# Self-attention in a fused network on Trainium2: row maxima sent in halves, the first quarter's high maxima made in its steps, k's first transfers on POOL's queue, half of the last batch finished in its steps

## The reference

```python
K = jnp.einsum('bse,hed->bhsd', xk, Wk)
V = jnp.einsum('bse,hed->bhsd', xv, Wv)
Q = jnp.einsum('bqe,hed->bhqd', xq, Wq)
scores = jnp.einsum('bhqd,bhkd->bhqk', Q, K)
scores = jnp.where(causal, -jnp.inf, scores)
att = jax.nn.softmax(scores / jnp.sqrt(jnp.asarray(sk, scores.dtype)), axis=-1)
out = jnp.einsum('bhqk,bhkd->bhqd', att, V)
...
return jax.nn.relu(out @ Wo + bo)
```

## Time and profile before

| | us |
|---|---|
| median of 3 runs | 2786.29 (2785.91 to 2787.86) |
| profiled execution | 2794.9 |
| its span | 2793.1 |
| PE busy | 2454.3 (88%) |
| DVE busy | 1614.1 (58%) |
| ACT busy | 1289.4 (46%) |
| POOL busy | 1321.1 (47%) |
| mean granted TensorE clock | 0.944 |
| self-attention, from its first instruction to the next stage's | 1042.4 to 1832.1 of the span |

### The profile page before, as it was taken

How to read it: one execution, slowest core, us unless ns; L and a number is a source line. 1 busy time by engine, 2 the same in 40 slices (tenths; PEclk the granted TensorE clock), 3 DMA queues, 4 the chain that set the end, 5 groups by cost and what they waited for, 6 DMA issues and landing times. The chain is left out here.

```text
span 2793.1 us, 42845 instructions
## 1 busy us (share of the span) xinstructions
PE 2454.3 (88%) x12770; PEld 1434.9 (51%) x12771; DVE 1614.1 (58%) x3230; ACT 1289.4 (46%) x2555; POOL 1321.1 (47%) x2216
## 2 busy tenths in 40 slices
...
DMA packets 85048, 115.13 MB, mean 41 GB/s; under 512 B 13880, under 2 KB 64160, under 8 KB 83072
## 3 DMA queue, kind: packets, MB, share of 16 engines
...
## 5 line engine op out<-in xcount | busy, mean ns | idle before, releaser
L3275 ACT ACTIVATE L2S_pT<-L2S_t_ps 128x512 f32<-128x512 f32 (+3 forms) x768 | 356.2, 490 | 251.4 <-PE L2S_t_ps L3102 243.9
L3339 DVE TENSOR_REDUCE L2S_mx<-L2S_s_ps 128x1 f32<-128x768 f32 (+7 forms) x384 | 351.4, 952 | 142.2 <-PE L2S_s_ps L3031 139.6
L3562 POOL TENSOR_SCALAR_AFFINE_SELECT L2S_pT<-L2S_pT 128x128 f32<-128x128 f32 x512 | 154.2, 310 | 374.9 <-ACT L2S_pT L3275 370.4
L3102 PE MATMUL L2S_t_ps<-L2S_q,L2S_k 98*128 98x512 bf16 (+3 forms) x768 | 254.5, 346 | 40.5 <-ACT L2S_pT L3275 24.1
L3030 PE MATMUL L2S_s_ps<-L2S_k,L2S_q 96*128 96x512 bf16 (+3 forms) x768 | 208.0, 344 | 29.7 <-DVE L2S_mx L3339 20.4
L622 POOL TENSOR_TENSOR L_prob<-L_prob,L_rc 128x616 f32<-128x616 f32 x64 | 82.3, 1287 | 231.3 <-DVE L_rc L555 231.3
L3102 PEld LDWEIGHTS L2S_t_ps<-L2S_q,L2S_k 98*128 98x128 bf16 x768 | 73.0, 99 | 227.1 <-ACT L2S_pT L3275 153.3
L3941 DVE TENSOR_TENSOR L3B_h<-L3B_si,L3B_u_ps 128x512 f32<-128x512 f32 x71 | 48.8, 688 | 237.9 <-PE L3B_u_ps L3884 213.0
L3858 POOL DMA_INDIRECT out<-L3B_y,L3F_rows x71 | 114.8, 1618 | 132.7 <-DVE L3B_y L3947 120.2
L3183 PE MATMUL L2S_o_ps<-L2S_pT,L2S_v 128*32 128x512 f32 (+3 forms) x1536 | 172.5, 524 | 0.0
L319 PE MATMUL L_scores<-weights,L_xT 128*128 128x308 f32 x512 | 143.1, 423 | 2.3 <-ACT L_xT L442 1.6
...
## 6 DMA issues: line engine op xcount, KB each, us to landing
...
```

The lines of the kernel that those rows point to most:

```text
L3102: nc.tensor.matmul(o[:, lo:512], k6[:, q % 2, j, kt * P:(kt + 1) * P], q6[:, q % 2, j, c * 512 + lo:(c + 1) * 512], start=True, stop=True) ...
L3275: nc.scalar.activation(pT[:, st % SLOTS, j, lo:512], t_ps[j % 2][:, lo:512], ACT.Exp, scale=SK).then_inc(s["exp_done"], 1)
L3339: nc.vector.tensor_reduce(dst, src, AX.X, ALU.max).then_inc(s["mx_done"], 1)
L3562: nc.gpsimd.affine_select(out=edge, in_=edge, compare_op=ALU.is_ge, fill=0.0, base=0, pattern=[[1, P]], channel_multiplier=-1).then_inc(s[ ...
```

## The change

1. `mx`, `mrow`, `q6` are laid out in two halves (low 512 queries, high 512), and `turn_max` has a half: the low half of the next quarter is turned at step 7, unit 3, the high half at step 1, unit 1 of the quarter itself. PE waits for the rows of a half only at that half's first unit (step 0, step 4).
2. In the prologue only the eight low maxima of quarter (0,0) are made; its sixteen high ones stand in steps 0 to 3 of the quarter, one per unit, and its high turn at step 3, unit 3. In that quarter the maxima of the next one go into steps 4 to 11, three each (FIRST_SHARE).
3. SHARE moves maxima from steps 6 and 7 to step 10. TURN_X moves by two units, PROJECT from steps (1: 5, 6, 8, 9; 2: 0, 3, 5, 8) to (1: 6, 8, 9, 11; 2: 5, 6, 8, 9).
4. k's first six writes and its first six loads are issued by POOL; SP waits for the writes before its loads of q. POOL's memset of k's rows of ones waits for all of xn instead of rstd.
5. In the last batch tiles 0 to 3 are transposed and multiplied by Wo at quarter 3, steps 8 to 11 (`end_turn`, `end_finish`), with residual and statistics by DVE; their rstd comes first in `last_walk`, their normalising after the last output turn, their scale and shift on POOL; they are sent by themselves. The end handles tiles 4 to 7.

The diff, cut to its core:

```diff
-    SHARE = (2, 2, 2, 2, 3, 3, 3, 3, 2, 2, 0, 0)
+    SHARE = (2, 2, 2, 2, 3, 3, 2, 2, 2, 2, 2, 0)
+    FIRST_SHARE = (0, 0, 0, 0, 3, 3, 3, 3, 3, 3, 3, 3)
     PEAK_AT = {0: (), 2: (0, 1), 3: (0, 1, 2)}
+    LAST_TURN_A = ((3, 8, 1), (3, 9, 1))
+    LAST_FINISH = ((3, 10), (3, 11))
     STATS = ((0, 1), (0, 3))
     NORM = ((1, 1), (1, 2))
-    TURN_X = ((1, 3, 0), (1, 3, 2), (1, 4, 0), (1, 4, 2))
-    PROJECT = ((1, 5), (1, 6), (1, 8), (1, 9), (2, 0), (2, 3), (2, 5), (2, 8))
+    TURN_X = ((1, 3, 2), (1, 4, 0), (1, 4, 2), (1, 5, 0))
+    PROJECT = ((1, 6), (1, 8), (1, 9), (1, 11), (2, 5), (2, 6), (2, 8), (2, 9))
...
-        q6 = sb("q6", [MR, 2, 4, S], BF16)
+        q6 = sb("q6", [MR, 2, 2, 4, 512], BF16)
...
-        mx = sb("mx", [P, 2, 4, TB])
-        mrow = sb("mrow", [4 * TB, 2, P], BF16)
+        mx = sb("mx", [P, 2, 2, 4, 4])
+        mrow = sb("mrow", [16, 2, 2, P], BF16)
...
-                    share, peaks = peaks[:SHARE[st]], peaks[SHARE[st]:]
+                    m = (FIRST_SHARE if first and q == 0 else SHARE)[st]
+                    share, peaks = peaks[:m], peaks[m:]
                     at = (q, st)
                     for j in range(4):
                         unit(q, st, j)
-                        for n, place in zip(share, PEAK_AT[SHARE[st]]):
+                        if first and q == 0 and st < 4:
+                            peak(0, TB + 4 * st + j)
+                        for n, place in zip(share, PEAK_AT[m]):
                             if place == j:
                                 peak(q + 1, n)
                         if (st, j) == (2, 2) and (q or not first):
                             turn_out(q - 1, 1)
                         if (st, j) == (7, 0):
                             turn_out(q, 0)
-                        if (st, j) == (10, 1) and (q + 1 < QUADS or more):
-                            turn_max(q + 1)
+                        if (st, j) == (7, 3) and (q + 1 < QUADS or more):
+                            turn_max(q + 1, 0)
+                        if (q, st, j) == (0, 3, 3) and first or (st, j) == (1, 1) and (q or not first):
+                            turn_max(q, 1)
...
+                        if not more:
+                            if (q, st, j) in LAST_TURN_A:
+                                end_turn(LAST_TURN_A.index((q, st, j)))
+                            if at in LAST_FINISH and j in (1, 2):
+                                end_finish(LAST_FINISH.index(at), j - 1)
...
-            for n in range(NP):
+            for n in range(TB):
                 peak(0, n)
-                if 1 <= n <= TB:
-                    first_v(n - 1)
-            turn_max(0)
+                first_v(n)
+            turn_max(0, 0)
...
+                sp.sem_inc(s["loaded_low0"], 48)
+                sp.sem_inc(s["loaded_high0"], 48)
                 write(0, 0, 0, 2)
-                write(0, 0, 1, 3)
+                sp.wait_ge(s["k_written"], 96)
+                sp.sem_inc(s["written1"], 96)
                 written(0, 0)
                 for q in range(2):
                     for cols, n in ((lowc, "low"), (highc, "high")):
-                        for which in "qk":
+                        for which in "qk" if q else "q":
...
+                for half, done in ((0, "a_half"), (1, "a_last")):
+                    sp.wait_ge(s[done], 1)
+                    chip.settle(sp)
+                    at = (B - 1) * TB + 4 * half
+                    sp.dma_start(dram["a"][:, at:at + 4, :], att[:, 4 * half:4 * half + 4, :]).then_inc(s["a_out"], 16)
+                sp.wait_ge(s["a_out"], 16 * B + 16)
...
+            def max_turned(q, half):
+                nc.tensor.transpose(r_ps[0:16, 0:P], mx[:, q % 2, half].rearrange("p h i -> p (h i)"), chip.ident[:]).then_inc(s["r_full"], 1)
...
-                    if st == 0 and j == 0:
-                        pe.wait_ge(s["mrow_in"], 32 * QUADS * b + 32 * (q + 1))
+                    if kt == 0 and j == 0:
+                        pe.wait_ge(s[f"mrow_in{c}"], 32 * QUADS * b + 32 * (q + 1))
...
+                def end_turn(dh):
+                    r.freed(pe, ("ea", dh))
+                    pe.wait_ge(s["r_dve"], r.dve(r.order.index(("o", QUADS - 1, 0)) + 1))
+                    for i in range(4):
+                        mm = nc.tensor.transpose(r_ps[:, i * P:(i + 1) * P], att[:, i, dh * P:(dh + 1) * P], chip.ident[:])
+                    mm.then_inc(s["r_full"], 1)
+
+                def end_finish(g, half):
+                    if half == 0:
+                        r.freed(pe, ("ef", g))
+                    if g == 0 and half == 0:
+                        pe.wait_ge(s["r_act"], r.act(r.order.index(("ea", 1)) + 1))
+                    for k in range(KD):
+                        t = 2 * g + half
+                        mm = nc.tensor.matmul(r_ps[:, half * D:(half + 1) * D], attT[:, k, t * P:(t + 1) * P], w["L2S_Wo"][:, k, :],
+                                              start=(k == 0), stop=(k == KD - 1))
+                    if half:
+                        mm.then_inc(s["r_full"], 1)
...
+                            mm = nc.tensor.transpose(s_ps[0][:, (4 * dh + i) * P:(4 * dh + i + 1) * P], att[:, 4 + i, dh * P:(dh + 1) * P], chip.ident[:])
+                    mm.then_inc(s["pre_full"], 1)
+                    pe.wait_ge(s["act_pre"], 11)
+                    for i in range(4):
+                        for k in range(KD):
+                            mm = nc.tensor.matmul(s_ps[1][:, i * D:(i + 1) * D], attT[:, k, (4 + i) * P:(5 + i) * P], w["L2S_Wo"][:, k, :],
+                                                  start=(k == 0), stop=(k == KD - 1))
+                        if i % 2:
+                            mm.then_inc(s["pre_full"], 1)
...
+                    dve.wait_ge(s["r_full"], r.full(("ef", g)))
+                    nc.vector.tensor_tensor(t, r_ps[:].rearrange("p (i d) -> p i d", d=D),
+                                            wide(chip.vec("L2_xattn_bo1").unsqueeze(1), [P, 2, D]), ALU.add).then_inc(s["r_dve"], 1)
+                    dve.wait_ge(s["r_dve"], r.dve(r.order.index(("ef", g)) + 1))
+                    dve.wait_ge(s["res_done"], 4 * B)
+                    rest_and_stats(t, 2 * g, end_step)
...
+                    pool.wait_ge(s["xn_done"], TB)
...
+                def project(m):
+                    if m:
+                        return
+                    pool.wait_ge(s["split_done"], 3)
+                    chip.settle(pool)
+                    for p in range(3):
+                        for qq in range(2):
+                            nc.gpsimd.dma_start(dram["parts"][1:2, qq, 2 - p, :, :, :].rearrange("o d h s -> (o d) h s"),
+                                                part[64 * qq:64 * qq + 64, 1, p, :]).then_inc(s["k_written"], 16)
+                    pool.wait_ge(s["k_written"], 96)
+                    chip.settle(pool)
+                    src = dram["parts"][1:2]
+                    for cols, n in ((slice(0, S // 2), 0), (slice(S // 2, S), 1)):
+                        for slot, count, p in ((0, 3, 0), (3, 2, 1), (5, 1, 2)):
+                            nc.gpsimd.dma_start(k6[slot * HD:(slot + count) * HD, 0, :, cols],
+                                                src[:, 0, p:p + count, :, :, cols].rearrange("o p d h s -> (o p d) h s")).then_inc(s[f"k_loaded{n}"], 16)
...
+                    pool.wait_ge(s["norm_y_done"], 2 * B - 1)
+                    chip.settle(pool)
+                    t = att[:, 0:4, :]
+                    nc.gpsimd.tensor_tensor(t, t, wide(chip.vec("L2_xattn_g1").unsqueeze(1), [P, 4, D]), ALU.mult).then_inc(s["scaled"], 1)
+                    pool.wait_ge(s["scaled"], 4 * B + 1)
+                    nc.gpsimd.tensor_tensor(t, t, wide(chip.vec("L2_xattn_b1").unsqueeze(1), [P, 4, D]), ALU.add).then_inc(s["a_half"], 1)
+                    power(rs_y, ve_y, mv_y, 1e-6, "stats_y_done", B + 1, "ve_y_done", "rstd_y_done", slice(4, 8))
```

191 lines of the change are left out of this document (103 added, 88 removed).

## The result

| | before | after |
|---|---|---|
| median, us | 2787.07 (4 runs, 2785.91 to 2791.12) | 2721.48 (4 runs, 2720.32 to 2722.98) |
| profiled execution, us | 2794.9 | 2722.25 |
| self-attention in it, us | 789.7 | 716.4 |
| mean granted clock | 0.944 | 0.957 |

The ratio is 0.9762, 95% interval 0.9746 to 0.9779: 65.6 us faster, where 37.9 were forecast. All of it is in the stage: 73.3 us less there in the profiled executions, 2.9 less ahead of it and 3.6 more behind. The difference of 7 us is spread over the stage, and most of it goes with the granted clock.

The account below looks back on a forecast made before the run. PE was taken to set the pace, joined by DVE where maxima are dense. -6.2 - 0.4 - 0.7 - 16.4 - 11 - 3.2 = -37.9 us (A to F) gave 2748.4 us, range 2738 to 2762, 8 in 10 2732 to 2771.

Parts of the forecast that it names:

- D: Quarters 2: later projections and turns of x end ACT's wait for SP's writes, -16.4 us, range -20 to -8.
- F: Last batch, half finished in its steps: end about 10 us shorter, steps +7, net -3.2 us, range -9 to +1.
- E: Quarters after the first: new shares and half turns give -11 us, range -20 to 0, with 4 set aside for r_ps.
- A: Prologue: with POOL's memset behind xn_done, eight normalising instructions take 3.2 instead of 9.4 us: -6.2, range -6.5 to -4.
- B: Prologue: k's first transfers on POOL's queue bring the first product of maxima -0.4 us, range -2.5 to +2.
- C: First quarter: high maxima moved into its steps, -15.7 + 11.7 + 3.3 = -0.7 us, range -7 to +7.
- (1): Rival: half the gain, D's stall moves to steps 5 and 6 and E gives nothing; -18.5, 2768 us, chance 0.19.
- (2): Rival: denser work in the half-clock stretches gets 2.4 GHz; C -7, D -20, F -9; 2733 us, chance 0.12.
- (3): Rival, slower: each of thirty-one turns waits for r_ps; decides from 2.5 us a quarter, at 2.9 2792 us; chance 0.05.
- (4): Rival: quarter 0 just moves its sixteen maxima, C +7 and B +2; -27.8, 2758 us, chance 0.62 together with the forecast.

Follow-up runs that it names:

- b_moved: Kernel before with only the new places of projections and turns of x (PROJECT, TURN_X): 2741.90 us, ratio 0.9859.
- b_again: Kernel before, unchanged, run once more for a second profile: 2783.53 us, with 782.6 us in the stage instead of 789.7.
- a_early_ones: Changed kernel with POOL's memset of k's rows of ones waiting for rstd again: 2730.07 us, ratio 0.9810.
- b_step2: Kernel before with the second half's projections moved from steps 0, 3, 5, 8 to 3, 5, 6, 8 of quarter 2: 2756.65 us, ratio 0.9903.
- b_both: Kernel before with the projection move of b_step2 and POOL's scale moved from quarter 2 to quarter 3: 2754.47 us, ratio 0.9895.
- b_clear: b_moved with POOL's scale and shift of the batch before moved from quarter 2 to quarter 3: 2738.07 us, ratio 0.9833.
- a_old_end: Changed kernel with the old end, all eight tiles of the last batch finished there in one transfer: 2730.13 us, ratio 0.9806.

## Why the forecast was too small

The direction was right; one step, D, was sized at under half, one term of F was three times too large and lay behind a difference of the clock, and E's sum was right by luck. By the stretches of the first section, with E read off as the difference between b_moved and the changed kernel (560.7 to 551.0):

| part | forecast | shown |
|---|---|---|
| A, B, C | -7.3 | -9.1 |
| D | -16.4 | -38.6 |
| E, with the collision that it took away | -11 | -9.7 |
| F, steps | +7 | -4.4 (at equal clock +2.3) |
| F, end | -10.2 | -11.5 (-10.4 from b_again) |

- **A** was right: 9.43 us of normalising are 2.67, and by a_early_ones the first unit moves by the same 6.7.
- **B** was right, by a cancelling of two things: POOL's issues (0.58 us, inside 0.5 to 0.9) are as many as SP's, and the first product now waits for q. The later first product costs nothing at the first unit. Of what the prediction cites from the Trainium skill (SBUF — State Buffer, the box on the "DVE blocks DMA" trap), that POOL's descriptors can't be written while a DVE instruction runs in a two-port mode, the trace shows nothing: six loads were issued in 3.46 us beside one cast of q's split (0.69 us), the six writes, with no DVE instruction beside them, in 3.45.
- **C** was right in both terms: first unit 22.3 us earlier forecast with A and B, 23.6 measured; quarter (0,0) +15.0 forecast, +14.5 measured. PE's wait at step 4 was 1.86 us, where a gap of 3 to 5 was expected.
- **D is the step that failed: "Its wait goes: -16.4 for three batches", with the range -20 to -8.** It took the wait's own row for the price of the stall, and the stall for all that the new places change. b_step2 shows 3.7, 8.5 and 10.1 us for the three stalls, 22.3 and not 16.4: in the two long ones steps 0 and 1 were 8.2 and 7.9 us longer, and part of what ran behind them did so at a lower clock (1.8 us in step 2 of (1,2)). The collision of split and scale, which the prediction named as what is "late next", was in the kernel before already (3.3 and 2.0 us on top in b_both), and is gone in the changed kernel, whose (1,2) takes 39.59. And "the moves (1,5) to (1,11) cost nothing" was wrong the other way: the first three quarters 1 got 9.1 us shorter in b_moved, 7.5 against b_again, in (1,1) at steps 3, 5 and 6 (0.8, 1.2 and 0.9 us). No run takes apart why. Two lengths in the trace had hinted at the size: quarter (1,2) takes 54.16 us, (3,2), with the same score work and nothing besides, 32.9. The excess of 21 us should have been shared out among its causes, the projections' own work too, before one of them was given 6.5; after the change 7.1 of it are left (39.59 against 32.51).
- The Trainium skill (SBUF — State Buffer, "Practical consequences") says that a cast can enter a two-port mode, in which it and a GpSimd instruction block each other, and that a tensor_tensor with both inputs in SBUF contends with a GpSimd instruction that reads SBUF. b_moved's trace agrees (0.43 becomes 1.14, 0.69 becomes 1.64); the prediction used the rule for the memset alone and not for the split.
- **E** was right in sum and not in kind. Of the 9.7 us from b_moved to the changed kernel 7.6 lie in (1,2) and (2,2), where the collision went away. From b_clear, which has none, it is 5.7 (556.8 to 551.0), half of the forecast. The relief of 1.5 us in each of the quarters 1 did not come: (0,1) takes 41.08 after 40.89, (1,1) 42.74 after 42.50. A quiet quarter got 0.4 us shorter ((3,2), 32.94 to 32.51) and not 0.8. Against the 4 us set aside for r_ps stand waits of PE of 6.9 us in nine turns.
- **F**: the end came as worked out, though a DVE instruction of 0.69 us took 2.51 beside POOL's shift. The steps did not pay 7 us but 2.3 or 2.4 at equal clock; the forecast took twice the work's own time and let little of it be hidden. Where the time is hidden no run shows. The other 6.7 us between +2.3 and -4.4 are the clock, 23.9 us at half in the profile of before and 3.4 in that of the changed kernel, and 0.50 was no constant of the place. What decides where the clock falls in (3,3) stays open: without the added work it was at half for 0 to 23.9 us in eight profiles, with it for 0 to 13.7 in nine.
- **Rivals.** (1), half the gain, fell: the split meets the scale in b_moved, as it says, and even so the quarter is 11 us shorter; in the changed kernel the two don't meet. (2), more by the clock, had the right sign, and its 2733 is nearer than the forecast, but by luck: C gave no 7 us, D is past its -20 and owes the clock about 1.8 us a quarter, and its F of -9 is met by a_old_end's 8.7 through added work that is cheap at either clock. (3), turns that wait for r_ps: the longest wait is 2.1 us and the mean 0.8, below the 2.5 from which it decides. (4), the first quarter at +7, fell: 52.7 us with its high maxima.

## What to carry to other kernels

Price a stall by the whole stretch against its twin that has none (here 54.2 against 32.9 us), not by the row of its wait: what is late behind it, a lower granted clock and an old collision are in the difference and in no single row. The difference is an upper bound, since the work that the twin lacks is in it too (7.1 of the 21 us stayed). Where DVE works from SBUF to SBUF, look what POOL runs in the same microseconds, also in the kernel before. A change of order on one in-order engine moves everything behind it: note what lands beside what. And before a slow stretch is given to a cause, profile the same kernel twice: here two executions differed by 7 us in this stage.

## What the runs showed of the chip

- A DVE cast, tensor_tensor or scalar_tensor_tensor from SBUF to SBUF that starts while a POOL tensor_tensor (1.3 or 2.3 us) runs ends just after it: a cast of 0.43 us took 1.14, a tensor_tensor of 0.69 took 1.64, a scalar_tensor_tensor of 0.69 took 2.51 when it met a POOL instruction of 2.34. Over the 17 profiles all 13 such casts of the split ended 0.28 to 0.29 us after the POOL instruction, all ten of its tensor_tensors 0.55 after it. DVE's reductions and subtractions out of PSUM beside the same POOL work kept their 0.69 to 0.96 us.
- POOL issues a transfer of 64 to 192 rows in 0.58 us, SP in 0.64; with k's transfers back on SP the first product came 1.3 us earlier and the first unit at the same time.
- The granted clock falls to half in pieces whose place and length differ between executions of one kernel: 13.6 and 23.9 us of it in the last quarter of two executions of before, 33.1 and 36.3 us long; with the same quarter's work and none of it the quarter takes 28.3 (b_moved, b_clear).
